# An S5 block with layer norms: the adds of Gelu and residual, moved from GpSimd to VectorE

## Chip, cores and metric

One core of a Trainium2 chip. The metric is the device time of one execution in microseconds (us); lower is better.

## The reference

`x` has 16 batches of 96 channels and 256 positions, in float32. Cut to what is computed:

```python
u = group_norm(x).transpose(0, 2, 1)             # 32 groups of 3 channels
fx = layernorm(u, ln1_g, ln1_b)
Bu = einsum('ph,blh->blp', B_bar, fx)            # 48 complex states
xs = associative_scan(h[t] = lam_bar * h[t-1] + Bu[t])
y = 2.0 * real(einsum('hp,blp->blh', Cc, xs)) + D * fx
y = gelu(y) + fx                                 # the add that the change moves
fy = layernorm(y, ln2_g, ln2_b)
z1, z2 = split(fy @ W_enc.T, 2, axis=-1)
y = (z1 * gelu(z2)) @ W_dec.T + fy
out = x + y.transpose(0, 2, 1)
```

## The kernel before

Channels lie on the 96 partitions. The 16 batches are two halves, H = 0 and 1; a half has 2048 columns, in NT = 4 tiles of 512, and tile i of half H has PSUM bank (H, i). Positions are sorted into T = 8 phases, so that the scan is seven steps between phases and a short doubling over the rest (`Z`). Each engine has its program written out by hand, one list of instructions in a fixed order with semaphore waits, and nothing reorders it. The halves are interleaved: while half 0 is in one stage, half 1 is in an earlier one.

The stages of a half that matter here, with the engine of each:
- TensorE writes the S5 outputs to PSUM: `direct`, `local_outputs`, and last `carried_outputs` (`Z,yl` matmuls in the trace).
- ScalarE takes Gelu of each tile: `gelu_y`, output `gl` (L379), semaphore `gl_ready`.
- The residual `fx` is added: `second_input`, `y2 = gl + fx`. On GpSimd (L290) for tiles 0 and 2 with semaphore `y2_pool`; on VectorE (L982) for tiles 1 and 3 with semaphore `y2_vec`. The inputs are read in order, the output is written with a step of 8 floats, since it goes back from phases to positions. In the trace the output is called `y`.
- TensorE centres y2: `center(H, i)` (`y,mt` matmuls), after it has waited for all four tiles. ScalarE makes `sq` and `xc` of it (`evacuate`), TensorE sums the squares (`variances`, `sq,mt`).
- VectorE works out the reciprocal root: `inverse_sigma(1, H)`, a chain of small instructions on `rs`, `upper` and `parts`. TensorE spreads it: `broadcast` (`parts,bcm`).
- VectorE scales: `scale_tile`, output `fy`, one instruction a tile with one operand from PSUM, semaphore `fy_ready`.
- TensorE's `encode` (`fy,mt`) needs two `fy` tiles for `encode(0, 0)` and four for the rest; then `gelu_z` on ScalarE, `gate` on VectorE (`w<-ps,vecs,y`), `decode` on TensorE, `finish` on VectorE (`sq<-ps,sm,res`), and a store.
- GpSimd makes `res = fy + x` for each tile: `residual` (L298), each waiting for its `fy`. It is the last thing on GpSimd, and in its list stands behind `second_input(1)`.

TensorE's list around the change, which the change leaves in this order:

```python
for i in range(NT - 1):
    direct(1, i); local_outputs(1, i)
pe.wait_ge(y2_pool, 2); pe.wait_ge(y2_vec, 2)
for i in range(NT):
    center(0, i); doubling(1, i)
...
    carried_outputs(1, i)
broadcast(1, 0)
encode(0, 0)
pe.wait_ge(y2_pool, 4); pe.wait_ge(y2_vec, 4)
for i in range(NT):
    center(1, i)
encode(0, 1)
```

Of the kernel before, what the change touches and what calls it, by code (L numbers as in the profile page):

```python
# [34 lines left out]
ALU = mybir.AluOpType  # L35
# [7 lines left out]
T = 8  # L43
# [5 lines left out]
NT = HC // TILE  # L49
RT = TILE // RC  # L50
# [38 lines left out]
def s5_block(nc, x, small, mats, mask_in, out):  # L89
    ctx = ExitStack()  # L90
    with ctx:
        def sb(name, shape, dt=F32):
            return ctx.enter_context(nc.sbuf_tensor(name, shape, dt))

        def sem(name):
            return ctx.enter_context(nc.semaphore(name))
# [3 lines left out]
        gl = sb("gl", [C, 2, HC])  # L100
        xc = sb("xc", [C, 2, HC])
        sq = sb("sq", [C, 2, HC])
        fx = sb("fx", [C + 1, 2, HC])
        w = sb("w", [P2, 2, HC])
        y2 = sb("y2", [C, 2, HC])
# [80 lines left out]
        z_ready = sem("z_ready")  # L186
        y_done = sem("y_done")
        gl_ready = sem("gl_ready")
        y2_pool = sem("y2_pool")
        y2_vec = sem("y2_vec")  # L190
        enc_done = sem("enc_done")
        gz_ready = sem("gz_ready")
# [9 lines left out]
        def cols(t, H, i, p=96):  # L202
            return t[0:p, H, TILE * i:TILE * (i + 1)]
# [7 lines left out]
        def s(c, n=1):  # L211
            return sm[:, c:c + n]

        def m(c, n=96):
            return mt[:, c:c + n]
# [7 lines left out]
        def tbl(k, n=NK, at=0):  # L223
            return tb[:, k, at:at + n]
# [14 lines left out]
        @block.sync  # L239
        def _(sp):  # L240
            for k, (first, last) in enumerate(LOADS):
                if last == B:
                    sp.dma_start(mt[:, N_EARLY:], mats[:, N_EARLY:]).then_inc(in_mats, 16)
                sp.dma_start(xs[:, first:last, :], x[:, first:last, :]).then_inc(in_x[k], 16)
            for n in range(2 * NT):
                H, i = divmod(n, NT)
                sp.wait_ge(out_ready, n + 1)
                sp.dma_start(out[:, 2 * n:2 * n + 2, :],
                             cols(ost, H, i).rearrange("c (n l) -> c n l", l=L)).then_inc(stored, 16)
            sp.wait_ge(stored, 16 * 2 * NT)  # L250

        @block.gpsimd
        def _(pool):
            n = [0]

            def chain(ins):
                n[0] += 1
                ins.then_inc(pool_chain, 1)

            def settle():  # L260
                pool.wait_ge(pool_chain, n[0])

            nc.gpsimd.memset(fx[96:97, :, :], 1.0).then_inc(ones_ready, 1)
            nc.gpsimd.memset(Z[:, :, :, 0:1], 0.0).then_inc(ones_ready, 1)

            pool.wait_ge(cos_ready, 1)
            nc.gpsimd.tensor_tensor(
                rotT[:, :, :], m(M_ID).unsqueeze(1).broadcast_to([96, T, 96]),
                tbl(COS, T).unsqueeze(2).broadcast_to([96, T, 96]), ALU.mult).then_inc(rotcos_ready, 1)
            pool.wait_ge(in_mats, 16)  # L270

            def combine(dst, mat_a, ca, mat_b, cb, n_mats):

                def mat(c):
                    return m(c).unsqueeze(1).broadcast_to([96, n_mats, 96])

                def coef(c):
                    return c.unsqueeze(2).broadcast_to([96, n_mats, 96])

                chain(nc.gpsimd.tensor_tensor(dst[:, 0], mat(mat_a), coef(ca), ALU.mult))  # L280
                chain(nc.gpsimd.tensor_tensor(dst[:, 1], mat(mat_b), coef(cb), ALU.mult))
                settle()
                return nc.gpsimd.tensor_tensor(dst[:, 0], dst[:, 0], dst[:, 1], ALU.add)

            def second_input(H):

                yv = y2[:, H, :].rearrange("c (m b) -> c b m", b=T)
                for i in (0, 2):
                    pool.wait_ge(gl_ready, NT * H + i + 1)
                    nc.gpsimd.tensor_tensor(  # L290
                        yv[:, RT * i:RT * (i + 1), :], cols(gl, H, i).rearrange("c (b m) -> c b m", b=RT),
                        cols(fx, H, i).rearrange("c (b m) -> c b m", b=RT), ALU.add).then_inc(y2_pool, 1)

            def residual(H):

                for i in range(NT):
                    pool.wait_ge(fy_ready, NT * H + i + 1)
                    nc.gpsimd.tensor_tensor(  # L298
                        cols(res, H, i), cols(fy, H, i),
                        xs[:, HB * H + 2 * i:HB * H + 2 * i + 2, :].rearrange("c n l -> c (n l)"),  # L300
                        ALU.add).then_inc(res_ready, 1)

            pool.wait_ge(tables_ready, 1)
            combine(rotX, M_ID, tbl(XCO, NX), M_SW, tbl(XSI, NX), NX).then_inc(rotx_ready, 1)
            combine(yl, M_C, tbl(CU, T), M_CS, tbl(SU, T), T).then_inc(yl_ready, 1)
            pool.wait_ge(yl_ready, 1)
            nc.gpsimd.tensor_tensor(yl[:, 1], yl[:, 0], tbl(RK, T).unsqueeze(2).broadcast_to([96, T, 96]),
                                    ALU.mult).then_inc(yl_ready, 1)
            for H in range(2):
                second_input(H)  # L310
                if H:
                    residual(0)
            residual(1)

        @block.scalar
# [106 lines left out]
        def _(pe):  # L422
# [103 lines left out]
            def local_outputs(H, i):  # L526
                for j in range(RT):
                    b = RT * i + j
                    if b:
                        pe.wait_ge(w_local[H], b)  # L530
                    mm(bank(H, i)[0:96, RC * j:RC * (j + 1)], yl[:, 0, b, :], rcols(w, H, b),
                       start=False, stop=False)
# [8 lines left out]
            def encode(H, i):  # L541

                if H == 0:

                    pe.wait_ge(fy_ready, (2, 4, 4, 4)[i])
                    if i == 2:
                        pe.wait_ge(taken[1], NT + 3)
                    if i == 3:
                        pe.wait_ge(taken[1], 2 * NT)
                        pe.wait_ge(var_read, 4)  # L550
                else:
                    pe.wait_ge(fy_ready, NT + i + 1)
                    pe.wait_ge(out_ready, (1, 2, 3, 4)[i])
                mm(bank(*Z1[H, i])[0:96, :], m(M_WE), cols(fy, H, i))
                mm(bank(*Z2[H, i])[0:96, :], m(M_WE + 96), cols(fy, H, i)).then_inc(enc_done, 1)
# [66 lines left out]
            for i in range(NT - 1):  # L622
                direct(1, i)
                local_outputs(1, i)
            pe.wait_ge(y2_pool, 2)
            pe.wait_ge(y2_vec, 2)
            for i in range(NT):
                center(0, i)
                doubling(1, i)
# [5 lines left out]
                carried_outputs(1, i)  # L635
            broadcast(1, 0)
            encode(0, 0)
            pe.wait_ge(y2_pool, 4)
            pe.wait_ge(y2_vec, 4)
            for i in range(NT):  # L640
                center(1, i)
            encode(0, 1)
# [19 lines left out]
        def _(dve):  # L662
# [168 lines left out]
            def statistics(H, q):  # L831

                for k, (first, _) in enumerate(LOADS):
                    if first == HB * H + q:
                        dve.wait_ge(in_x[k], 16)
                nc.vector.bn_stats(st[:, HB * H + q, :], xs[:, HB * H + q, :]).then_inc(gn_stats, 1)  # L836
# [73 lines left out]
            def scale_tile(k, H, i, dst, gain, ready):  # L910

                dve.wait_ge(inv_bcast[k], NT * H + i + 1)
                stt(cols(dst, H, i), cols(xc, H, i), gain, bank(H, i)[0:96, :],
                    ALU.mult, ALU.mult).then_inc(ready, 1)

            def scan(H, b):

                dve.wait_ge(u_done, NT * H + b // RT + 1)
                if b == 1:
                    dve.wait_ge(w_first, H + 1)  # L920
                else:
                    dve.wait_ge(w_local[H], b - 1)
                stt(rcols(w, H, b), rcols(w, H, b - 1), tbl(RK, 1, 1),
                    bank(H, b // RT)[0:96, RC * (b % RT):RC * (b % RT + 1)],
                    ALU.mult, ALU.add).then_inc(w_local[H], 1)
# [52 lines left out]
            def second_input(H, i):  # L978

                dve.wait_ge(gl_ready, NT * H + i + 1)  # L980
                yv = y2[:, H, :].rearrange("c (m b) -> c b m", b=T)
                nc.vector.tensor_tensor(  # L982
                    yv[:, RT * i:RT * (i + 1), :], cols(gl, H, i).rearrange("c (b m) -> c b m", b=RT),
                    cols(fx, H, i).rearrange("c (b m) -> c b m", b=RT), ALU.add).then_inc(y2_vec, 1)
# [10 lines left out]
                doubled(0, i)  # L995
            for b in range(1, T):
                scan(1, b)
            second_input(0, 1)
            second_input(0, 3)
            for k in range(NDBL):  # L1000
                doubled(1, k)
            inverse_sigma(1, 0)
            second_input(1, 1)
            for i in range(NT):
                if i == 2:
                    second_input(1, 3)
                scale_tile(1, 0, i, fy, s(G2), fy_ready)
            dve.wait_ge(vecs_ready, 1)
            gate(0, 0)
# [78 lines left out]
```

## Time and profile before

| | us |
|---|---|
| runs shown | 110.52, 117.62, 116.42 (median 116.42) |
| the profiled execution's own time | 110.42 |
| its span, first to last instruction | 108.6 |
| TensorE busy | 94.9 |
| VectorE busy | 77.6 |
| ScalarE busy | 41.0 |
| GpSimd busy | 31.9 |

The span is what the profile covers; 1.8 us of the execution's time lie around it. In the rows PE is TensorE's matmuls, PEld its weight loads, DVE VectorE, ACT ScalarE, POOL GpSimd. `L664` and `L424` are lines of helpers that record many operations, so an instruction is told by its tiles. A matmul of float32 operands appears as two instructions. Times are from the span's start.

### The profile page before, as it was taken

To read this page: it belongs to the slowest core of one execution; us is meant where nothing else is said; L and a number is where in the kernel's file an instruction comes from. 1 tells how busy PE (TensorE), PEld (TensorE's weight loads), DVE (VectorE), ACT (ScalarE), POOL (GpSimd) and SP (SyncE) were. 2 spreads that over 40 slices of the span, in tenths; PEclk is the share of its full clock that TensorE was granted. 3 is DMA by queue.
4 is the path that set the end of the run, shared out by engine and by line. 5 is a ranking of instruction groups with operands and counts; after the bars stand their busy time and mean duration, and the time that the engine had idled before them with its cause. 6 is when DMAs were issued, how large, how long until landed. Compare 5 with 4: busy or idle time off the path is not lost.

```text
span 108.6 us, 1488 instructions
## 1 busy us (share of the span) xinstructions
PE 94.9 (87%) x502; PEld 56.2 (52%) x502; DVE 77.6 (71%) x260; ACT 41.0 (38%) x79; POOL 31.9 (29%) x26
## 2 busy tenths in 40 slices
PE   5999897269989929999899999999599999999960
PEld 4668766146555715676476655567324432533310
DVE  1688999999986899658677302389990289994590
ACT  2254167807449100024037009818049722024200
POOL 8600000400049992000018000007995000296000
PEclk9999999955799999999999999999999999999997
DMA  2997000000000000000000000000000000450135
GB/s 77 275 262 168 3 0 0 6 0 0 0 0 0 0 0 3 0 6 0 0 0 0 0 0 3 6 0 0 0 0 0 0 0 0 118 149 29 28 84 177
DMA packets 3767, 3.79 MB, mean 35 GB/s; under 512 B 496, under 2 KB 3664, under 8 KB 3760
## 3 DMA queue, kind: packets, MB, share of 16 engines
q1 hardware_dynamic: 3392, 3.49, 12.3%
q10 hardware_dynamic: 368, 0.20, 0.8%
q8 instruction: 4, 0.07, 0.3%
q14 instruction: 3, 0.02, 0.1%
HBM read 2.12 MB, written 1.57 MB: 34 GB/s over the span
## 4 chain that ended last, share of the span: by engine, by line
PE 70%; DVE 21%; issue 4%; ACT 1%; DVEq 1%
PE ps L424 70%; DVE st L836 2%; DVE fy L664 2%; DVE pm L885 2%; DVE sc L694 2%; DVE rs L664 1%; DVE upper L668 1%; DVE sq L664 1%; DVE tb L664 1%; DVE tb L668 1%; DVE y L982 1%; DVE gn L664 1%; DVE rs L694 1%; DVE fx L664 1%; DVE sc L664 1%
## 5 line engine op out<-in xcount | busy, mean ns | idle before, releaser
L424 PE MATMUL ps<-fy,mt 96*96 96x512 f32 x32 | 14.9, 600 | 1.3 <-DVE fy L664 1.3
L290 POOL TENSOR_TENSOR y<-gl,fx 96x512 f32<-96x512 f32 x4 | 6.1, 1524 | 29.8 <-ACT gl L379 29.8
L298 POOL TENSOR_TENSOR res<-fy,xs 96x512 f32<-96x512 f32 x8 | 10.7, 1359 | 11.6 <-DVE fy L664 11.5
L424 PE MATMUL ps<-xs,pm 96*96 96x256 f32 x32 | 10.8, 492 | 3.3 <-DVE pm L885 3.3
L385 ACT ACTIVATE y<-ps,vecs 96x512 f32<-96x512 f32 x8 | 5.5, 687 | 16.4 <-PE ps L424 16.4
L664 DVE SCALAR_TENSOR_TENSOR w<-ps,vecs,y 96x512 f32<-96x512 f32 x8 | 5.9, 743 | 7.4 <-ACT y L385 7.4
L424 PE MATMUL ps<-fx,dm 96*96 96x512 f32 x16 | 8.4, 605 | 2.6 <-issue 2.2
L933 DVE TENSOR_TENSOR Z<-Z,ps 96x240 f32<-96x240 f32 (+3 forms) x8 | 2.8, 355 | 9.5 <-PE ps L424 9.5
L424 PEld LDWEIGHTS ps<-fy,mt 96*96 96x96 f32 x32 | 5.0, 163 | 8.7 <-issue 6.8
L424 PEld LDWEIGHTS ps<-xs,pm 96*96 96x96 f32 x32 | 6.4, 214 | 5.9 <-DVE pm L885 3.8
L379 ACT ACTIVATE gl<-ps,db 96x512 f32<-96x512 f32 x8 | 5.5, 684 | 9.4 <-PE ps L424 9.4
L424 PE MATMUL ps<-wm 96*96 96x256 f32 x20 | 7.9, 586 | 1.2 <-DVE wm L949 1.2
L424 PE MATMUL ps<-fx,um 97*96 97x256 f32 x32 | 8.2, 390 | 0.2 <-DVE fx L664 0.2
L424 PE MATMUL ps<-w,yl 96*96 96x256 f32 x32 | 8.2, 379 | 0.0
L664 DVE SCALAR_TENSOR_TENSOR w<-w,tb,ps 96x256 f32<-96x256 f32 x14 | 6.6, 471 | 1.9 <-ACT w L366 1.2
L424 PE MATMUL ps<-w,mt 96*96 96x512 f32 x16 | 7.8, 602 | 0.0
L424 PEld LDWEIGHTS ps<-w,yl 96*96 96x96 f32 x32 | 5.2, 163 | 5.1 <-issue 4.0
L358 ACT ACTIVATE sq<-ps,vecs 96x512 f32<-96x512 f32 x8 | 5.5, 686 | 6.2 <-PE ps L424 6.2
L424 PE MATMUL ps<-y,mt 96*96 96x512 f32 x16 | 7.7, 595 | 0.1
L340 ACT ACTIVATE sq<-ps,gn 96x256 f32<-96x256 f32 x16 | 6.5, 470 | 2.7 <-PE ps L424 2.6
L424 PE MATMUL ps<-Z,yl 96*96 96x256 f32 x32 | 7.2, 379 | 0.0
L424 PEld LDWEIGHTS ps<-wm 96*96 96x96 f32 x20 | 5.1, 262 | 3.6 <-DVE wm L949 1.2
(112 smaller groups left out, 168.1 us busy)
## 6 DMA issues: line engine op xcount, KB each, us to landing
out_dram<-sq SPq DMA_DIRECT2D x8, 192.0 KB, 2.2
xs<-x_dram SPq DMA_DIRECT2D x3, 384.0 KB, 6.1
xs<-x_dram SPq DMA_DIRECT2D x2, 192.0 KB, 3.5
mt<-mats_dram SPq DMA_DIRECT2D x1, 338.6 KB, 6.8
mt<-mats_dram ACTq DMA_DIRECT2D x1, 180.0 KB, 3.9
sm<-small_dram ACTq DMA_DIRECT2D x1, 8.6 KB, 2.8
cmask<-mask_dram ACTq DMA_DIRECT2D x1, 9.0 KB, 4.9
```

Of the source, the lines that this page charges most:

```text
L290: nc.gpsimd.tensor_tensor(yv[:, RT * i:RT * (i + 1), :], cols(gl, H, i).rearrange("c (b m) -> c b m", b=RT), cols(fx, H, i).rearrange("c ( ...
L298: nc.gpsimd.tensor_tensor(cols(res, H, i), cols(fy, H, i), xs[:, HB * H + 2 * i:HB * H + 2 * i + 2, :].rearrange("c n l -> c (n l)"), ALU. ...
L340: nc.scalar.activation(t[:, H, :].rearrange("c (b n a) -> c n b a", b=T, n=HB)[:, n], bank(H, n // 2)[0:96, L * (n % 2):L * (n % 2 + 1)].r ...
L358: nc.scalar.activation(cols(sq, H, i), bank(H, i)[0:96, :], ACT.Square, bias=vecs[:, 2:3]).then_inc(squared[1], 1)
L379: nc.scalar.activation(cols(gl, H, i), bank(H, i)[0:96, :], ACT.Gelu, bias=db[:, 0:1]).then_inc(gl_ready, 1)
L385: nc.scalar.activation(cols(gz, H, i), bank(*Z2[H, i])[0:96, :], ACT.Gelu, bias=vecs[:, 1:2]).then_inc(gz_ready, 1)
L424: return nc.tensor.matmul(o, lhsT, rhs, start=start, stop=stop)
L664: return nc.vector.scalar_tensor_tensor(out=o, in0=a, scalar=sca, in1=b, op0=op0, op1=op1)
L668: return nc.vector.tensor_scalar(o, a, s1, None, op0)
L694: self.add(nc.vector.tensor_tensor(*a))
L836: nc.vector.bn_stats(st[:, HB * H + q, :], xs[:, HB * H + q, :]).then_inc(gn_stats, 1)
L933: nc.vector.tensor_tensor(zd, zd, o[:, :, d:], ALU.add).then_inc(z_ready, 1)
```

## The change

VectorE makes all eight y2 tiles. In half 0 it makes the four one after another behind the scan of half 1; in half 1 it makes tile 0 ahead of the first `scale_tile`, and tiles 1, 2 and 3 each ahead of the `scale_tile` with the same number. GpSimd keeps only `residual`, without a `second_input` ahead of it. The semaphore `y2_pool` goes, and TensorE waits for counts 4 and 8 of `y2_vec`. `second_input(H, i)` itself is the same code.

```diff
-            def second_input(H):
-
-                yv = y2[:, H, :].rearrange("c (m b) -> c b m", b=T)
-                for i in (0, 2):
-                    pool.wait_ge(gl_ready, NT * H + i + 1)
-                    nc.gpsimd.tensor_tensor(
-                        yv[:, RT * i:RT * (i + 1), :], cols(gl, H, i).rearrange("c (b m) -> c b m", b=RT),
-                        cols(fx, H, i).rearrange("c (b m) -> c b m", b=RT), ALU.add).then_inc(y2_pool, 1)
...
-            for H in range(2):
-                second_input(H)
-                if H:
-                    residual(0)
+            residual(0)
             residual(1)
...
-            pe.wait_ge(y2_pool, 2)
-            pe.wait_ge(y2_vec, 2)
+            pe.wait_ge(y2_vec, 4)
             for i in range(NT):
                 center(0, i)
                 doubling(1, i)
...
             encode(0, 0)
-            pe.wait_ge(y2_pool, 4)
-            pe.wait_ge(y2_vec, 4)
+            pe.wait_ge(y2_vec, 8)
             for i in range(NT):
                 center(1, i)
...
             for b in range(1, T):
                 scan(1, b)
-            second_input(0, 1)
-            second_input(0, 3)
+            for i in range(NT):
+                second_input(0, i)
             for k in range(NDBL):
                 doubled(1, k)
             inverse_sigma(1, 0)
-            second_input(1, 1)
-            for i in range(NT):
-                if i == 2:
-                    second_input(1, 3)
+            second_input(1, 0)
+            for i in range(NT):
+                if i:
+                    second_input(1, i)
                 scale_tile(1, 0, i, fy, s(G2), fy_ready)
             dve.wait_ge(vecs_ready, 1)
             gate(0, 0)
```

VectorE's list from the end of `inverse_sigma(1, 0)` (output `parts`) to the first two gates (output `w`), before:

```order
L668 TENSOR_SCALAR upper<-rs 128x128
L664 SCALAR_TENSOR_TENSOR parts<-upper,cmask,rs 128x128
L982 TENSOR_TENSOR y<-gl,fx 96x2x256
L664 SCALAR_TENSOR_TENSOR fy<-xc,sm,ps 96x512 x2
L982 TENSOR_TENSOR y<-gl,fx 96x2x256
L664 SCALAR_TENSOR_TENSOR fy<-xc,sm,ps 96x512 x2
L664 SCALAR_TENSOR_TENSOR w<-ps,vecs,y 96x512 x2
```

The same place after the change (`y<-gl,fx` is `second_input`, now L967; `fy` is `scale_tile`):

```order
L649 SCALAR_TENSOR_TENSOR parts<-upper,cmask,rs 128x128
L967 TENSOR_TENSOR y<-gl,fx 96x2x256
L649 SCALAR_TENSOR_TENSOR fy<-xc,sm,ps 96x512
L967 TENSOR_TENSOR y<-gl,fx 96x2x256
L649 SCALAR_TENSOR_TENSOR fy<-xc,sm,ps 96x512
L967 TENSOR_TENSOR y<-gl,fx 96x2x256
L649 SCALAR_TENSOR_TENSOR fy<-xc,sm,ps 96x512
L967 TENSOR_TENSOR y<-gl,fx 96x2x256
L649 SCALAR_TENSOR_TENSOR fy<-xc,sm,ps 96x512
L649 SCALAR_TENSOR_TENSOR w<-ps,vecs,y 96x512 x2
```

The two adds have become four, and each `fy` but the first has an add right ahead of it.

GpSimd's list from its last table product to its end, before (`yl` are tables of the first stage):

```order
L281 TENSOR_TENSOR yl<-mt,tb 96x768
L283 TENSOR_TENSOR yl<-yl 96x768
L307 TENSOR_TENSOR yl<-yl,tb 96x768
L290 TENSOR_TENSOR y<-gl,fx 96x2x256 x4
L298 TENSOR_TENSOR res<-fy,xs 96x512 x8
```

And after:

```order
L279 TENSOR_TENSOR yl<-mt,tb 96x768
L280 TENSOR_TENSOR yl<-mt,tb 96x768
L282 TENSOR_TENSOR yl<-yl 96x768
L297 TENSOR_TENSOR yl<-yl,tb 96x768
L288 TENSOR_TENSOR res<-fy,xs 96x512 x8
```

The four adds are gone, and the first `res` has only the wait for its `fy` ahead of it.

## Rows read from the trace of the kernel before

**Rows 1.** The page, busy time, share of the span and instructions by engine.

```profile
PE 94.9 (87%) x502; PEld 56.2 (52%) x502; DVE 77.6 (71%) x260; ACT 41.0 (38%) x79; POOL 31.9 (29%) x26
```

**Rows 2.** The chain that ended last, in order: start us, us, what.

```profile
73.75 1.25 DVE upper L668
...
79.71 12.55 PE ps L424 x58
```

**Rows 3.** Timeline, half 0: start us, us, engine line op out<-in [idle before <-releaser].

```profile
56.53 1.28 POOL L290 TENSOR_TENSOR y<-gl,fx 96x512 f32<-96x512 f32 x1 [15.03 <-ACT gl L379]
...
57.35 1.41 DVE L982 TENSOR_TENSOR y<-gl,fx 96x512 f32<-96x512 f32 x1 [0.63 <-ACT gl L379]
...
59.08 1.63 DVE L982 TENSOR_TENSOR y<-gl,fx 96x512 f32<-96x512 f32 x1 [0.32 <-ACT gl L379]
...
64.15 1.02 PE L424 MATMUL ps<-y,mt 96*96 96x512 f32 x2
```

**Rows 4.** Timeline, half 1, 72 to 80 us.

```profile
72.68 2.75 PE L424 MATMUL ps<-Z,yl 96*96 96x256 f32 x12
...
73.02 0.23 DVE L668 TENSOR_SCALAR upper<-rs 128x128 bf16<-128x128 f32 x1
...
73.64 1.28 POOL L290 TENSOR_TENSOR y<-gl,fx 96x512 f32<-96x512 f32 x1 [13.87 <-ACT gl L379]
...
73.75 1.24 DVE L668 TENSOR_SCALAR upper<-rs 128x128 bf16<-128x128 f32 x1
...
75.30 1.09 DVE L982 TENSOR_TENSOR y<-gl,fx 96x512 f32<-96x512 f32 x1
75.36 2.03 POOL L290 TENSOR_TENSOR y<-gl,fx 96x512 f32<-96x512 f32 x1 [0.45 <-ACT gl L379]
...
75.44 1.09 PE L424 MATMUL ps<-parts,bcm 128*96 128x128 bf16 x16
...
76.23 1.38 DVE L664 SCALAR_TENSOR_TENSOR fy<-xc,sm,ps 96x512 f32<-96x512 f32 x2
77.35 3.22 POOL L298 TENSOR_TENSOR res<-fy,xs 96x512 f32<-96x512 f32 x2
77.53 2.03 DVE L982 TENSOR_TENSOR y<-gl,fx 96x512 f32<-96x512 f32 x1
...
77.66 1.96 PE L424 MATMUL ps<-fy,mt 96*96 96x512 f32 x4 [1.13 <-DVE fy L664]
...
79.41 0.71 DVE L664 SCALAR_TENSOR_TENSOR fy<-xc,sm,ps 96x512 f32<-96x512 f32 x1
```

**Rows 5.** Instructions by tile (count: shortest/median/longest ns); last, `fy` (us, mean ns).

```profile
L982 DVE TENSOR_TENSOR y<-gl,fx x4: 1091/1516/2032, 57.4 to 77.5; 96x512 f32<-96x512 f32 x4
...
L290 POOL TENSOR_TENSOR y<-gl,fx x4: 1277/1392/2034, 56.5 to 75.4; 96x512 f32<-96x512 f32 x4
...
L298 POOL TENSOR_TENSOR res<-fy,xs x8: 1265/1268/1997, 77.4 to 98.3; 96x512 f32<-96x512 f32 x8
...
L664 DVE SCALAR_TENSOR_TENSOR fy<-xc,sm,ps 96x512 f32<-96x512 f32 x8 | 5.6, 731 | 0.1
```

**Rows 6.** Timeline, the same stage of half 1 in the second layer norm.

```profile
93.23 1.06 PE L424 MATMUL ps<-parts,bcm 128*96 128x128 bf16 x16
...
93.66 0.74 DVE L664 SCALAR_TENSOR_TENSOR fy<-xc,sm,ps 96x512 f32<-96x512 f32 x1
...
94.48 2.59 POOL L298 TENSOR_TENSOR res<-fy,xs 96x512 f32<-96x512 f32 x2 [11.45 <-DVE fy L664]
```

**Rows 7.** Stretches: us, PE busy (instructions), granted clock, DMA share, GB/s.

```profile
20.00:22.00 2.00, 0.00 (x0) 0.94 0.00 0
...
22.00:28.00 6.00, 5.34 (x14) 0.50 0.00 0
...
38.00:40.00 2.00, 0.00 (x0) 1.00 0.00 0
```

**Rows 8.** Timeline, TensorE behind its idle time of 38 to 40 us.

```profile
40.05 1.07 PE L424 MATMUL ps<-fx,dm 96*96 96x512 f32 x2 [2.21 <-issue]
```

More of the change, by code:

```diff
@@ L188, in s5_block @@
         gl_ready = sem("gl_ready")
-        y2_pool = sem("y2_pool")
         y2_vec = sem("y2_vec")
```

## The prediction, made before the changed kernel was run

> **What bounds the kernel now.** I read the page's line of busy times first, then the chain of waits, then the timeline around the two places where y2 is made, and last the granted clock. TensorE is busy 94.9 us of the 108.6 us span [rows 1], so whatever does not delay TensorE costs nothing. The chain [rows 2] names the places where it is not TensorE: one of them is VectorE from 73.75 us to 77.6 us (the end of `inverse_sigma(1, 0)`, an add, two `fy` tiles). After it the chain is TensorE alone for 12.55 us from 79.71 us. So a delay at 79.71 us, the start of `center(1, 0)`, has no idle time behind it that could swallow it, and goes to the end in full. `center(1, 0)` waits for all four adds of half 1; that wait is the term to work out.
>
> **Half 0 of the change: nothing.** In before, two adds of half 0 run on GpSimd and two on VectorE, the last ending at 59.08 + 1.63 = 60.71 us, and TensorE starts `center(0, 0)` at 64.15 us because its own queue gets there only then [rows 3]: 3.4 us of cover. After, VectorE is free of scans at 56.72 us (57.35 less its 0.63 us of idle time), and the last Gelu tile is there by 59.08 us, where VectorE's add had waited for it. Four uncontended adds at 0.93 us from start to start (worked out below) from 56.7 us end at about 60.6 us. I cost this half at 0; the cover would be gone only if an add took over twice its 1.09 us. The replaced semaphore (one wait for two) costs nothing either, since it is met early.
>
> **The price of an add.** The four adds on VectorE took 1.09 to 2.03 us and those on GpSimd 1.28 to 2.03 [rows 5], and the long ones lie over one another [rows 3, 4]. VectorE's add at 57.35 us starts while GpSimd runs until 56.53 + 1.28 = 57.81, and ends at 58.76, 0.95 us after that. The one at 77.53 us starts in GpSimd's first `res` (77.35 + 1.27 = 78.62, 1.27 being the median of rows 5) and ends at 79.56, 0.94 us after. In the other direction GpSimd's add at 75.36 us starts 0.06 us behind VectorE's of 75.30, and ends at 77.40, 1.01 us after VectorE's end. So of two such instructions the later one is held until the first is over, then needs 0.94 us (VectorE) or 1.01 us (GpSimd). An add on VectorE held by nobody is the 1.09 us one at 75.30; the next instruction starts 0.93 us after it, at 76.23, and 0.15 us before a held one's end (79.56, 79.41). The `fy` tiles, with one operand from PSUM, are not held: two in 1.38 us beside GpSimd's add at 76.23, 0.73 us each with starts 0.65 apart.
>
> The Trainium skill states the same ("SBUF — State Buffer", section Who interferes with whom): a VectorE instruction with two SBUF inputs and a GpSimd instruction that reads SBUF exclude each other for a whole instruction, the first to issue winning. The trace agrees, with the 0.94, 0.95 and 1.01 us above.
>
> **Half 1, what goes.** GpSimd's adds at 73.64 and 75.36 us disappear. The first of them held VectorE's `upper` for 1.24 us, where its like at 73.02 took 0.23 [rows 4]. So `parts` is ready at 74.37 us and not 75.38. But that 1.01 us is not won: TensorE is busy with the sixteen `Z,yl` matmuls (twelve of them in 2.75 us, 0.216 apart, the last starting at 75.05), and the broadcast, now at 75.44, can begin one step behind them, at 75.27. The gain is 0.17 us. The first `fy` can then start 0.43 us later, as in the second round (93.23 to 93.66) [rows 6], at 75.70 us. The first add of half 1 fits in front of it, from 74.30 to 75.39, in time that VectorE would otherwise wait.
>
> **Half 1, what comes.** VectorE's order is now fy, add, fy, add, fy, add, fy where it was add, fy, fy, add, fy, fy, with the wait of `center(1, 0)` on the last add. GpSimd, idle at that time, can start `res` as soon as the first `fy` is there, 0.08 us behind its end (93.66 + 0.74 = 94.40, and 94.48) [rows 6], and each `res` reads two SBUF tiles. Step by step, in us:
> - fy 0 from 75.70 to 76.43. Add 1 issues at 76.35 and has SBUF first: to 77.44. `res` 0 issues at 76.51, is held, and ends at 77.44 + 1.01 = 78.45.
> - fy 1 from 77.28 to 78.01. TensorE's `encode(0, 0)` starts at 78.06, now 77.66.
> - Add 2 issues at 77.93, is held by `res` 0 and ends at 78.45 + 0.94 = 79.39. `res` 1 is held by it and ends at 80.40.
> - fy 2 from 79.24 to 79.97. Add 3 issues at 79.89, is held by `res` 1 and ends at 80.40 + 0.94 = 81.34.
> - `center(1, 0)` starts 0.15 us after the last add (79.56 [rows 4] and 79.71 [rows 2]): 81.49, against 79.71. That is 1.78 us later.
> fy 3 starts 0.15 us before the end of add 3 and ends at 81.92 us, early enough for `encode(0, 1)`, which comes behind the eight matmuls of `center(1, i)`, not before 83 us. `gate(0, 0)` and the rest of VectorE's and GpSimd's work move with TensorE. TensorE is idle for about 1.5 us before 78.06 and again for 1.7 us before 81.49.
>
> **Sum.** 0 (half 0) + 1.78 (half 1) = 1.8 us. The profiled execution took 110.42 us for a span of 108.6; I expect a span of 110.4 and a time of 112.2 us. That is 1.6%; about 2% is what a measurement of this kernel can tell from no change. Of the three runs shown one (110.52) lies with the profiled execution, two (116.42, 117.62) are 6 to 7 us above it, and the profile does not show what makes them so; the median, 116.42, is one of these. The change adds the same 1.8 us there, 118.2. I name the level at which the rows were taken, and let the range reach the other.
>
> **Bounds of the price.** Above: GpSimd wins each time, see below. Below: if no add were held, the adds and `fy` tiles follow from 75.70 at 0.65 and 0.93 us, add 3 runs from 79.51 to 80.60, and `center(1, 0)` starts at 80.75, 1.04 us late. If besides an add cost only what an `fy` tile does (0.73, the nearest row with 96x512 elements [rows 5]), add 3 runs from 78.95 to 79.68 and the loss is 0.12 us. A gain is excluded here: two adds more stand ahead of the wait, one of them between fy 0 and fy 1 on which `encode(0, 0)` waits, and the broadcast moves only 0.17 us. I take 1.78, because both ingredients (0.94 after a holder, 1.01 after a holder) were each seen in before with the same instructions.
>
> The Trainium skill has a rule that would give that lowest case ("GPSIMD Engine Reference", section 4.1 Engine selection): elementwise work of two inputs belongs on VectorE, GpSimd being about twice as slow. By it an add would cost half of 1.27 us, 0.64, and the loss would be about 0.1 us. The trace does not agree: 1.09 us on VectorE against 1.28 on GpSimd. A reason is in "Advanced Engine Details and Errata", section SBUF Cachelines: accesses that each land in another 16-byte line pay a penalty, and this add writes y2 with a step of 32 bytes.
>
> **The rivals.**
> - *Adds without collisions, or short ones.* GpSimd's `res` doesn't get in between, or the adds are cheap: +0.1 to +1.0 us, 110.5 to 111.5. For it: uncontended adds exist. Against: nothing else occupies GpSimd, and `fy` is ready before every add.
> - *GpSimd wins the collisions* (the slower side). `res` 0 issues 0.16 us behind add 1; if GpSimd still gets SBUF first, `res` 0 runs to 77.78, add 1 to 78.72, fy 1 to 79.30; `res` 1 from 79.38 to 80.65, add 2 to 81.59, fy 2 to 82.17; `res` 2 from 82.25 to 83.52, add 3 to 84.46; `center(1, 0)` at 84.61, 4.9 us late: 115.3 us. It decides from one lost collision on (some 1.3 us each). Against it stands the pair at 75.30 and 75.36, where a lead of 0.06 us was enough for VectorE.
> - *The clock falls.* TensorE's granted clock fell once to half (1.2 of 2.4 GHz), shortly before 22 us, in a stretch of 2 us without a matmul, and was there from 22 to 28 us. The 2.21 us of idle time before 40.05 left it at full [rows 7, 8]. If it fell after the two idle stretches around 80 us for as long, 6 us, it would cost half of that, 3 us more: 115.2.
> - *The change helps.* The 1.01 us taken off `upper` would have to reach TensorE; it reaches it with 0.17. Faster by more than 2% needs 2.2 us, and no row has them.
>
> **How the numbers follow.** The forecast, two held adds of three: 0.58, own range 111.6 to 112.8. Without collisions or short: 0.20. GpSimd first: 0.11. Clock: 0.07. Helps: 0.04. The 2% bound lies 2.2 us above the profiled 110.42. The forecast's upper tail over it is about 0.10, with the two rivals 0.28 slower; 0.04 faster; 0.68 within 2%. The range goes from 110.6 to 118.8: from the case without collisions, over the slower rivals, to the upper level of executions, 118.2 and a little.
>
> **What would show it.** In the profile after: `upper` at 0.23 us both times; the broadcast within 0.2 us of 75.27; VectorE's adds in half 0 at about 1.09 us each, and in half 1 two of four at about 1.5 us; GpSimd's first two `res` near 2 us; TensorE idle twice between 76.3 and 81.5 us; `center(1, 0)` at 81.5. If `center(1, 0)` starts before 80.8 us the collisions didn't happen, if after 82.5 GpSimd wins them; a granted clock of 0.50 behind 80 us would speak for the third rival. Any difference before 55 us would be none of this change's.

## The result, and the profile after

| | executions | us |
|---|---|---|
| before, in the comparison on record | 4 | 110.52, 110.80, 116.42, 117.62 |
| changed | 4 | 114.41, 114.48, 114.61, 114.86 (median 114.55) |
| ratio on record | | 1.0355, interval 1.0312 to 1.0398 |
| before, all jobs of this study | 78 | mean 112.75 ± 0.19, median 112.4, 110.2 to 118.1 |
| changed, all jobs | 25 | mean 114.49 ± 0.19, median 114.6, 112.6 to 116.4 |

The ratio on record compares only executions within 1.5% of the lowest of their kernel, and of the kernel before that left two, 110.52 and 110.80. By it the change costs 3.9 us; by all executions 1.74 ± 0.27 us in the mean (1.5%) and 2.2 in the median (± is the standard error of a mean). The same ratio in the three later jobs that ran both kernels is 1.022 (interval 1.014 to 1.030), 1.013 (1.006 to 1.021) and 1.018 (1.001 to 1.035). A job is one batch of executions on one chip. The prediction had 1.8 us. The measured time was inside its range; its forecast that the change would stay within 2% did not hold by the ratio on record.

The profiled execution took 114.41 us for a span of 112.6, 4.0 us more than before. The chain of waits of the changed kernel, in order of time (start us, us, what), stands against [rows 2]:

```profile
40.66 8.13 PE ps L411 x26
...
77.99 0.74 DVE fy L649
78.73 0.99 DVE y L967
79.72 0.56 DVE fy L649
80.28 1.39 DVE y L967
81.67 0.56 DVE fy L649
82.23 1.40 DVE y L967
83.62 0.04 issue
83.67 12.58 PE ps L411 x58
```

VectorE's fy and add in turn have become the chain, and TensorE's long piece of 12.55 us is still 12.58 us long, only later. The timeline of the same place answers to [rows 4]:

```profile
74.11 3.62 PE L411 MATMUL ps<-Z,yl 96*96 96x256 f32 x16
...
76.05 0.23 DVE L653 TENSOR_SCALAR upper<-rs 128x128 bf16<-128x128 f32 x1
...
76.58 1.07 DVE L967 TENSOR_TENSOR y<-gl,fx 96x512 f32<-96x512 f32 x1
...
77.56 1.06 PE L411 MATMUL ps<-parts,bcm 128*96 128x128 bf16 x16
...
77.99 0.74 DVE L649 SCALAR_TENSOR_TENSOR fy<-xc,sm,ps 96x512 f32<-96x512 f32 x1 [0.34 <-PE ps L411]
78.65 1.07 DVE L967 TENSOR_TENSOR y<-gl,fx 96x512 f32<-96x512 f32 x1
78.81 7.03 POOL L288 TENSOR_TENSOR res<-fy,xs 96x512 f32<-96x512 f32 x4 [36.71 <-DVE fy L649]
...
80.20 1.47 DVE L967 TENSOR_TENSOR y<-gl,fx 96x512 f32<-96x512 f32 x1
80.33 1.96 PE L411 MATMUL ps<-fy,mt 96*96 96x512 f32 x4 [1.72 <-DVE fy L649]
...
82.15 1.46 DVE L967 TENSOR_TENSOR y<-gl,fx 96x512 f32<-96x512 f32 x1
...
83.67 1.53 PE L411 MATMUL ps<-y,mt 96*96 96x512 f32 x3 [1.37 <-DVE y L967]
```

`upper` is back at 0.23 us, two adds take 1.07 us and two 1.46 to 1.47, GpSimd's four `res` take 7.03 us where four free ones are 5.1, and TensorE is idle twice, 1.72 and 1.37 us.

Three distances place the 4.0 us. E runs from the span's start to the first `Z,yl` matmul of half 1, ahead of everything changed in half 1. D runs from there to `center(1, 0)`, the changed stretch. The tail is the rest.

| us | E | D | tail |
|---|---|---|---|
| before | 71.81 | 7.90 | 28.92 |
| changed | 74.11 | 9.56 | 28.96 |

D has 1.66 us of the loss, E has 2.30. Ahead of the end of E the two profiles differ in two ways. VectorE waited longer for the input (before first, changed second; start us, us, what):

```profile
6.69 0.42 DVE L836 BATCH_NORM_STATS2 st<-xs 96x6 f32<-96x256 f32 x1 [0.45 <-DMA xs<-x_dram]
```

```profile
7.77 0.42 DVE L821 BATCH_NORM_STATS2 st<-xs 96x6 f32<-96x256 f32 x1 [1.28 <-DMA xs<-x_dram]
```

Further on, TensorE's first `fx,dm` matmul starts 0.6 us later than the 40.05 of [rows 8]:

```profile
40.66 1.07 PE L411 MATMUL ps<-fx,dm 96*96 96x512 f32 x2 [3.19 <-issue]
```

The later input is the likely cause of these 0.6 us; no run tests it. And the granted clock was low at another time (stretches: us, PE busy, granted clock; before first, changed second):

```profile
20.00:30.00 10.00, 7.34 (x35) 0.66 0.00 0
30.00:40.00 10.00, 7.54 (x58) 1.00 0.00 0
40.00:50.00 10.00, 9.78 (x51) 1.00 0.01 2
```

```profile
20.00:30.00 10.00, 6.97 (x47) 0.83 0.01 2
30.00:40.00 10.00, 7.17 (x58) 1.00 0.00 0
40.00:50.00 10.00, 9.18 (x40) 0.83 0.01 2
```

Before, the half clock (1.2 GHz) lay between 20 and 30 us: 0.34 of 10 us off the mean are 6.8 us at half clock. Changed, the same 6.8 us lay in two parts, between 20 and 30 us and between 10 and 20, where the mean was also 0.83. A further part lay between 40 and 50, and from 40.66 us on TensorE has hardly any idle time there: 0.17 of 10 us are 3.4 us at half clock, and half of those, 1.7 us, are lost. From `fx,dm` to the end of E took 31.76 us before and 33.45 changed, 1.7 us more. So 0.6 + 1.7 = 2.3 us is E's difference. Whether the change has a part in it was the question for the runs.

### The profile page after: what moved, and what is told of

It reads as the page before. It is cut to its first block, busy times and chain, and to the rows that moved or that the text cites. A ratio compares the mean times of both kernels' runs of the same rounds, so it can differ in the third digit from the quotient of the medians.

```text
span 112.6 us, 1486 instructions
## 1 busy us (share of the span) xinstructions
PE 96.7 (86%) x502; PEld 57.5 (51%) x502; DVE 79.4 (71%) x264; ACT 40.8 (36%) x79; POOL 27.2 (24%) x22
## 4 chain that ended last, share of the span: by engine, by line
PE 65%; DVE 19%; DMA 5%; issue 5%; ACT 1%; SPq 1%; DVEq 1%
PE ps L411 65%; DMA xs<-x_dram 5%; DVE y L967 3%; DVE fy L649 2%; DVE rotT L649 1%; DVE pm L870 1%; DVE sc L679 1%; DVE st L821 1%; DVE rs L649 1%; DVE sq L649 1%; SPq L243 1%; DVE fx L649 1%; DVE sc L649 1%; ACT y L372 1%; DVEq L91 1%
## 5 line engine op out<-in xcount | busy, mean ns | idle before, releaser
L288 POOL TENSOR_TENSOR res<-fy,xs 96x512 f32<-96x512 f32 x8 | 12.1, 1530 | 49.4 <-DVE fy L649 49.3
L411 PE MATMUL ps<-fx,dm 96*96 96x512 f32 x16 | 9.3, 663 | 3.6 <-issue 3.2
L411 PE MATMUL ps<-xs,pm 96*96 96x256 f32 x32 | 9.6, 450 | 2.8 <-DVE pm L870 2.8
L411 PE MATMUL ps<-w,yl 96*96 96x256 f32 x32 | 9.1, 411 | 0.0
L967 DVE TENSOR_TENSOR y<-gl,fx 96x512 f32<-96x512 f32 x8 | 9.0, 1182 | 0.0
L411 PEld LDWEIGHTS ps<-w,yl 96*96 96x96 f32 x32 | 5.7, 178 | 5.9 <-issue 4.9
L411 PEld LDWEIGHTS ps<-xs,pm 96*96 96x96 f32 x32 | 5.8, 193 | 5.0 <-DVE pm L870 3.1
L649 DVE SCALAR_TENSOR_TENSOR fx<-xc,sm,ps 96x512 f32<-96x512 f32 x8 | 5.6, 737 | 3.3 <-PE ps L411 3.3
L821 DVE BATCH_NORM_STATS2 st<-xs 96x6 f32<-96x256 f32 x16 | 6.5, 418 | 1.3 <-DMA xs<-x_dram 1.3
```

Of the source, the lines that this page charges most:

```text
L288: nc.gpsimd.tensor_tensor(cols(res, H, i), cols(fy, H, i), xs[:, HB * H + 2 * i:HB * H + 2 * i + 2, :].rearrange("c n l -> c (n l)"), ALU. ...
L411: return nc.tensor.matmul(o, lhsT, rhs, start=start, stop=stop)
L649: return nc.vector.scalar_tensor_tensor(out=o, in0=a, scalar=sca, in1=b, op0=op0, op1=op1)
L967: nc.vector.tensor_tensor(yv[:, RT * i:RT * (i + 1), :], cols(gl, H, i).rearrange("c (b m) -> c b m", b=RT), cols(fx, H, i).rearrange("c ( ...
```

## The experiments

**The changed kernel again.** No edit.

> The changed kernel once more, nothing edited. Two distances in the profile tell the causes apart. D is from the first Z,yl matmul of half 1 to center(1, 0): 7.90 us before, 9.56 us after. E is from the span's start to that Z,yl matmul, all of it ahead of the changed instructions of half 1: 71.81 us before, 74.11 us after. Theory A (the change itself costs D alone, +1.7 us, and the rest of the loss is where TensorE's clock happened to be low and when the input landed in the one execution): D is 9.5 to 9.6 again, E moves by over 0.5 us from 74.11, times spread. Theory B (the change also slows the first part): E is 74.1 within 0.2 us, the ratio to the kernel before stays near 1.035.

Six executions, mean 114.83 us against 112.25 for 18 of the kernel before in the same job, and the ratio on record fell to 1.022. E was 71.69, even less than before, with the half clock at the place where the kernel before had it (mean 0.66 from 20 to 30 us, 1.00 from 30 to 50), and D 9.56. So E's 2.3 us are not the change's, theory A, and half 0 of the change costs nothing ahead of the end of E either. But the profiled time was 114.42 us again, for another reason, in TensorE's timeline and clock at 80 us:

```profile
77.92 2.15 PE L411 MATMUL ps<-fy,mt 96*96 96x512 f32 x4 [1.71 <-DVE fy L649]
81.25 6.21 PE L411 MATMUL ps<-y,mt 96*96 96x512 f32 x8 [1.19 <-DVE y L967]
87.29 1.88 PE L411 MATMUL ps<-fy,mt 96*96 96x512 f32 x4
```

```profile
79.00:81.00 2.00, 1.06 (x3) 0.64 0.00 0
81.00:83.00 2.00, 1.75 (x2) 0.50 0.00 0
83.00:85.00 2.00, 2.00 (x4) 0.50 0.00 0
85.00:87.00 2.00, 2.00 (x4) 0.65 0.00 0
```

The eight matmuls of `center(1, i)` took 6.21 us where they take 3.67. The clock had fallen between TensorE's two idle stretches: a mean of 0.64 from 79 to 81 us puts the fall at 79.6 us. That is 1.6 us after the first idle stretch had ended and 0.5 us ahead of the second, in the `fy,mt` matmuls, which took 2.15 us for 1.96. The tail was 31.29 us: 2.3 more. This is the prediction's third rival, except that only one of the two idle stretches lay ahead of the fall.

**Half the change each.** `half0` is the kernel before with this edit (the counts of TensorE's waits follow):

```diff
-            for H in range(2):
-                second_input(H)
-                if H:
-                    residual(0)
+            second_input(1)
+            residual(0)
             residual(1)
...
-            second_input(0, 1)
-            second_input(0, 3)
+            for i in range(NT):
+                second_input(0, i)
```

`half1` leaves half 0 to both engines and has the change's loop in half 1:

```diff
-            second_input(1, 1)
+            second_input(1, 0)
             for i in range(NT):
-                if i == 2:
-                    second_input(1, 3)
+                if i:
+                    second_input(1, i)
                 scale_tile(1, 0, i, fy, s(G2), fy_ready)
```

> Only half 0 of the change: VectorE makes the four tiles of half 0, half 1 as before. Theory A: D stays 7.9 us, the time is that of the kernel before in its lower executions, 110.5 to 111, and E is what clock and input give. Theory B, if the cause lies in half 0: time near 112.8 to 113, E near 74.1, D 7.9.

> Only half 1 of the change: VectorE makes the four tiles of half 1 and GpSimd those of half 0 as before. Theory A: D is 9.5 to 9.6 us, times as for the full change. Theory B, if the cause lies in half 0: D 9.5 and time near 112.2.

`half0`: D 7.89 us, tail 28.99, ten executions from 110.41 to 114.48, mean 113.03 ± 0.45 against 112.25 ± 0.30 for the kernel before, and not the 110.5 to 111 us expected. The difference of 0.8 is under two of its own errors, so the mean settles little; D settles it. E was 75.79 in this profile, with the clock at half in two places ahead of 50 us. `half1`: D 9.56 us, E 73.52, mean 114.68 of four, and no half clock at 80 us though TensorE had the same two idle stretches, 1.72 and 1.37 us. The whole of D's growth comes from half 1.

**The residual out of the way.**

```diff
+            pool.wait_ge(y2_vec, 8)
             residual(0)
             residual(1)
```

> The changed kernel, with GpSimd's first residual held back until all y2 tiles are there, so that no res instruction lies over an add. If the held adds are worth what the prediction took (0.46 us each, with 0.27 us more at the third add than the uncontended chain), D falls from 9.56 to about 8.95 (center(1, 0) 1.04 us later than before and not 1.7), adds all at 1.09 us, and the time falls by 0.6 to 0.75 us against the changed kernel. Rival: the order of VectorE's list alone sets D and it stays at 9.5. The res tiles come about 5 us later, which has cover until the first finish.

D 8.78 us, a little below the 8.95 expected. VectorE's part of the timeline in this profile:

```profile
77.10 0.74 DVE L650 SCALAR_TENSOR_TENSOR fy<-xc,sm,ps 96x512 f32<-96x512 f32 x1 [0.33 <-PE ps L412]
77.76 1.07 DVE L968 TENSOR_TENSOR y<-gl,fx 96x512 f32<-96x512 f32 x1
78.67 0.73 DVE L650 SCALAR_TENSOR_TENSOR fy<-xc,sm,ps 96x512 f32<-96x512 f32 x1
79.31 1.08 DVE L968 TENSOR_TENSOR y<-gl,fx 96x512 f32<-96x512 f32 x1
80.22 0.73 DVE L650 SCALAR_TENSOR_TENSOR fy<-xc,sm,ps 96x512 f32<-96x512 f32 x1
80.87 1.08 DVE L968 TENSOR_TENSOR y<-gl,fx 96x512 f32<-96x512 f32 x1
```

Every add is at 1.07 or 1.08 us, so the two long ones came from GpSimd's `res` and cost 9.56 - 8.78 = 0.78 us. The remaining 0.88 us over the 7.90 of before is left to the order of the list; the last experiment tests that. Four executions, 112.91 to 116.71, say nothing finer.

**The write in order.** Left out is the rearrangement from phases to positions; y2 has its columns in another order, and what follows is computed on that.

```diff
-                    yv[:, RT * i:RT * (i + 1), :], cols(gl, H, i)...
+                    cols(y2, H, i).rearrange("c (b m) -> c b m", b=RT), cols(gl, H, i)...
```

> The changed kernel with the adds' output written in order instead of with a step of 8 floats; the rearrangement from phases to positions is left out, so y2 has its columns in another order and everything behind it is computed on that. Theory (the step of 32 bytes makes the add 1.09 us long): uncontended adds take 0.70 to 0.75 us, D falls by 0.6 to 1.1 us from 9.56, since two adds are still held by a res. Rival (two inputs from SBUF make the add long): adds stay at 1.09.

By tile, in this profile (count: shortest/median/longest ns):

```profile
L967 DVE TENSOR_TENSOR y<-gl,fx x8: 679/686/1095, 57.4 to 80.0; 96x512 f32<-96x512 f32 x8
...
L288 POOL TENSOR_TENSOR res<-fy,xs x8: 1255/1269/1719, 77.2 to 99.8; 96x512 f32<-96x512 f32 x8
```

A free add took 0.68 us, the last two, beside GpSimd's `res`, 1.09, and D was 8.63. The step of 32 bytes in the output is worth 0.4 us an add on VectorE; two inputs from SBUF alone don't make it long. This is one execution.

**TensorE kept busy at 80 us.** The changed kernel with dummy matmuls into a free bank:

```diff
+            pe.wait_ge(gl_ready, NT + 1)
+            keep_busy(3, bank(1, 0))        # 3 x mm(free[0:96, 0:256], wm[:, 0:96], wm)
             encode(0, 0)
+            keep_busy(3, bank(1, 0))
             pe.wait_ge(y2_vec, 8)
```

> The changed kernel with six dummy matmul calls (256 columns, float32, 0.43 us each) in TensorE's two idle stretches, three behind broadcast(1, 0) and three behind encode(0, 0), so that TensorE is not idle there. Clock theory (the clock falls to half in part of the executions because of these two stretches, as in the second profile of the changed kernel, where that cost 2.4 us): no stretch of clock 0.50 between 60 us and the end in any profile, D within 0.3 us of 9.56, and the mean over executions falls by 0.5 to 1.5 us against the changed kernel's. Rival (the fall at 80 us is rare and the changed kernel's surplus lies ahead of 60 us): mean unchanged within 0.3 us, or worse by the matmuls.

> The changed kernel with six dummy matmul calls in the two idle stretches, again. Clock theory: no clock 0.50 between 60 us and the end, mean 1.2 to 2 us above the kernel before (D's share alone, 1.66), below the changed kernel.

> The changed kernel once more, in one job with the filled one. So far D has been 9.55 and 9.56 us in its two profiles, and the clock fell at 79.6 us in one of them. Clock theory: mean over the executions 0.5 to 1.5 us above the filled kernel's in this job, and 2 to 3 us above the kernel before; D 9.5 to 9.6. Rival: no difference to the filled kernel beyond 0.3 us.

In both profiles D was 9.58 to 9.59, the tail 28.93 to 28.96, with no half clock behind 60 us. `again2`, unfilled, had D 9.56 and the fall at 81.6 us (tail 31.17). The means: filled 113.99 and 114.20 us in two jobs of twelve executions, together 114.09 ± 0.26; changed 114.49 ± 0.19. The difference of 0.40 ± 0.32 has the expected sign and is not clear of noise. What was expected of the means in that job failed: the changed kernel was 1.0 us above the kernel before (114.42 against 113.38 of 17) and not 2 to 3, and 0.2 above the filled one and not 0.5 or more; the filled one was 0.8 above the kernel before and not 1.2 to 2.

**How often the clock falls there.**

> The changed kernel, one profile more. D 9.5 to 9.6 us. If the clock falls near 80 us, the distance from center(1, 0) to the end of the span is 31.3 us and not 28.9; I expect this in one profile of three.

> The changed kernel, a third job. D 9.56 us. If the clock falls near 80 us in about half of the executions, as in two of four profiles so far, the mean is 2.8 us above the kernel before; if in a quarter, 2.2; if the fall is an accident of two profiles, 1.7.

> One profile more of the changed kernel, for the share of executions in which the clock falls near 80 us: center(1, 0) to the end 28.9 us without a fall, 31.2 with it; D 9.56.

> One profile more of the changed kernel, as the run before it.

> The kernel before, one profile more. D 7.9 us, no clock fall between 60 us and the end, 28.9 us from center(1, 0) to the end; E anywhere from 71.7 to 76 us, with the early clock falls at other places than in the first profile.

| profile | E | D | tail |
|---|---|---|---|
| changed | 74.11 | 9.56 | 28.96 |
| again | 71.69 | 9.56 | 31.29 |
| again2 | 73.92 | 9.56 | 31.17 |
| again3 | 75.26 | 9.56 | 28.93 |
| again4 | 74.40 | 9.56 | 28.95 |
| again5 | 73.30 | 9.56 | 28.99 |
| again6 | 72.77 | 9.56 | 28.96 |
| before | 71.81 | 7.90 | 28.92 |
| before2 | 74.90 | 7.90 | 28.90 |

Two of seven profiles of the changed kernel have the fall at 80 us, neither of the kernel before. In `again2` (mean 0.66 from 81 to 83 us) it lies as in `again`: 1.5 us after the first idle stretch, in the `fy,mt` matmuls (2.31 us for 1.96), ahead of the second stretch. With `half1`, which has the same two stretches, it is two of eight. D is the same to 0.01 us in each. E goes from 71.7 to 75.3 with the changed kernel and from 71.8 to 74.9 with the kernel before: the two overlap. Two of seven times 2.3 us are 0.6 us on average, which with D's 1.66 gives 2.3 us. The pooled means have 1.74 ± 0.27 and the medians 2.2. `again4` (mean 114.36 of six, the kernel before 112.39 of 16 in that job) lies between the lower two of its three cases. `before2` shows besides that the kernel before falls to half clock at `fx,dm` too, the place where the prediction saw it stay at full [rows 7, 8]:

```profile
40.04 1.99 PE L424 MATMUL ps<-fx,dm 96*96 96x512 f32 x2 [1.88 <-issue]
```

```profile
40.00:50.00 10.00, 9.96 (x37) 0.68 0.01 2
```

The idle time was 1.88 us here, shorter than the 2.21 us of the first profile.

**The early idle time filled.** The kernel before, with dummy matmuls in the idle stretches that end at 22.66 and 40.05 us:

```diff
                 variances(0, 0, i)
+            pe.wait_ge(bias_ready, 1)
+            keep_busy(5, bank(1, 1))
             center_batch(1, 0)
...
+            pe.wait_ge(taken[0], 2 * HB)
+            keep_busy(4, bank(1, 3))
             pe.wait_ge(dm_ready, 1)
```

> The kernel before with dummy matmul calls of the same kind in its two early idle stretches: five behind the variances of half 0 (idle 2.9 us before 22.66), four ahead of the wait for the output tables (idle 2.2 us before 40.05). If the scatter of both kernels (E from 71.7 to 75.8 us in the profiles) comes from clock falls after these two stretches, the executions draw together near the lowest, 108 to 110.5 us, and the profile has no 0.50 between 15 and 60 us. Rival (the scatter comes from when the input lands): it stays at 3 us and more.

Four of six executions were at 110.02 to 111.40, the others 116.82 and 122.28. The profile was of the longest:

```profile
19.00:36.00 17.00, 17.00 (x82) 0.51 0.01 1
36.00:53.00 17.00, 17.00 (x66) 0.50 0.01 1
53.00:60.00 7.00, 6.83 (x39) 0.98 0.00 0
```

TensorE's rows show a matmul all the time, and the clock stayed at half for 34 us. So the expectation failed: four executions drew together, but all except one above the 108 to 110.5 us expected, and the fall that the dummies were to prevent came all the same, in matmuls, soon after 19 us. The ratio on record is 0.988 (interval 0.981 to 0.995), from the low executions; the mean of all six is 113.7 us. E was 83.61 us in this profile against 71.81. TensorE's matmuls at 17 us began only 0.24 us later than in the profile of before, so nearly all of the 11.8 us come from the half clock and the dummies themselves, not from the input.

**Another order.** VectorE: add, add, fy, fy, add, add, fy, fy; `residual` behind all adds, as above.

```diff
-            second_input(1, 0)
             for i in range(NT):
-                if i:
+                if i % 2 == 0:
                     second_input(1, i)
+                    second_input(1, i + 1)
                 scale_tile(1, 0, i, fy, s(G2), fy_ready)
```

> The changed kernel with VectorE's half 1 in the order add, add, fy, fy, add, add, fy, fy, and GpSimd's residual behind all adds. Theory (the order of the list and the held adds make D): encode(0, 0) waits for fy 1 only, as before; add 3 ends 7.67 us after the first Z,yl matmul and D is 7.8 to 7.9, so TensorE is idle once, for 1.2 us, and the clock stays up at 80 us; the time is that of the kernel before within 0.5 us, 1.5 to 3 us below the changed kernel. Rival: four adds on VectorE cost by their number, D stays above 8.7 as with the residual held back alone.

> The order add, add, fy, fy again, in one job with the changed kernel. Theory (D and the idle time at 80 us are all that the change costs): D 7.7 us, no clock fall between 60 us and the end, mean over the executions that of the kernel before within 0.5 us and 1.5 to 2.5 us below the changed kernel's in the same job. Rival (VectorE's eight adds cost something outside D): mean above the kernel before by over 0.5 us.

Timeline of `pairs`:

```profile
74.05 3.62 PE L412 MATMUL ps<-Z,yl 96*96 96x256 f32 x16
...
76.51 2.02 DVE L968 TENSOR_TENSOR y<-gl,fx 96x512 f32<-96x512 f32 x2
...
78.37 1.38 DVE L650 SCALAR_TENSOR_TENSOR fy<-xc,sm,ps 96x512 f32<-96x512 f32 x2
79.67 2.01 DVE L968 TENSOR_TENSOR y<-gl,fx 96x512 f32<-96x512 f32 x2
79.80 1.96 PE L412 MATMUL ps<-fy,mt 96*96 96x512 f32 x4 [1.25 <-DVE fy L650]
...
81.74 3.67 PE L412 MATMUL ps<-y,mt 96*96 96x512 f32 x8
```

D 7.70 and 7.69 us in the two profiles, 0.2 below the kernel before, though VectorE makes all eight tiles. `pairs` had expected 7.8 to 7.9. Against the 8.78 of `res_late`, which differs in the order alone, one `fy` fewer (0.65 us from start to start) stands ahead of the last add, and the second add uses the 0.33 us in which VectorE waited for the broadcast: together 0.98 of the 1.08 us. TensorE is idle only ahead of `fy,mt`. 24 executions have a mean of 112.50 ± 0.24 us, 2.0 ± 0.3 below the changed kernel and 0.25 ± 0.3 below the kernel before. The ratios to the kernel before were 0.9958 (0.990 to 1.001) and 1.0072 (1.002 to 1.012) in the two jobs. It is no faster than the kernel before by any amount that can be measured; it undoes the loss. The rival, a cost of over 0.5 us of VectorE's eight adds outside D, falls: in the job of `pairs2` the mean was 112.50 us against 112.39 for the kernel before.

## Why the prediction was right or wrong

- *Half 0 costs nothing*: right in the profile. The four adds took 3.89 us from 58.94, all near 1.1 us, and `center(0, 0)` started at 66.44, 3.6 us after them. `half0` left D at 7.89. One reading was off: four adds from 56.7 us use up the cover until 64.15 when an add takes about 1.95 us, not "over twice its 1.09".
- *`upper` gives 1.01 us to VectorE and 0.17 to TensorE*: right. It took 0.23 us; the broadcast came 3.45 us after the first `Z,yl`, before 3.63.
- *The price of an add and who holds whom*: right. Free adds 1.07, held ones 1.46 and 1.47 (forecast 1.46 and 1.45 by its own start and end times), VectorE first at add 1. `res_late` took the collisions away and got 0.78 us back, where the prediction's own bound said 0.74.
- *`center(1, 0)` 1.78 us late*: D says 1.66. The term was 0.12 us too large, most of it because `center(1, 0)` began 0.06 us after the last add's end (83.61 and 83.67) and not 0.15. The rival in which GpSimd wins the collisions, 4.9 us, did not come in any profile.
- *Adds at half of GpSimd's price, no collisions*: by the trace no. `plain_write` shows what that rival's low price needs: an output in order, 0.68 us. The Trainium skill ("Advanced Engine Details and Errata", section SBUF Cachelines) states a penalty for accesses that each land in another 16-byte line. The run agrees, with 1.07 us at a step of 32 bytes against 0.68.
- *The tail moves as a whole*: right where the clock stays up, 28.9 us in every such profile.
- *The clock rival*: this is a step that failed. It was held to 0.07, from one idle stretch of 2.21 us that left the clock at full. That row was one draw: in `before2` the clock fell at the same place around a stretch of 1.88 us. At 80 us it fell in two of seven profiles, in the matmuls behind the first idle stretch of 1.7 us. It costs 2.2 to 2.3 us, less than the 3 of the prediction.
- *The level*: the other step that failed, and the one on which "0.68 within 2%" rested. The sum set its 1.8 us on 110.42 us, the profiled execution, and put what differs between executions ahead of 55 us at nothing, but for an upper level of 116 to 118 that it left unexplained. 78 executions of the kernel before have a median of 112.4 us; 110.42 is below all but three of them. 72 of them fill the stretch from 110.2 to 114.5 without a gap, and only six lie at 116.3 to 118.1. Where profiles exist (E from 71.7 to 75.8, `fill_early` aside), the half clock lay at different times ahead of 50 us, and the changed kernel has the same scatter. In the comparison on record, four executions of it at 114.4 to 114.9, none near its own lowest of 112.59, stood against two of before that are among the lowest eight of 78. That makes 3.9 us of a difference that is 1.7 to 2.3. For the profiled execution the rest is E's 2.3 us; the other three have no profile, so what made them long stays open.

So the mechanism and the size of its term stood. That the measured time fell into a range 8.2 us wide, 110.6 to 118.8, says little for them; D says more. Whether the change is within 2% depends on which executions are compared: 1.5% by the means, 2.0% by the medians, 3.6% by the ratio on record, 1.3 to 2.2% by the same ratio in the later jobs.

Open: why the clock falls at 80 us in some executions only, and how often beyond two in seven. The second idle stretch is not what makes it fall, since both falls came ahead of it. That the first, longer than in the kernel before (1.72 against 1.13 us), is needed is argued and not shown: it rests on filled profiles without a fall (two), on profiles of `pairs` (two) and of before (two), and with a share of two in seven, six profiles without a fall could also be chance. The gain of the filled kernel, 0.40 ± 0.32 us, doesn't settle it.

## What to carry to other kernels

Moving work to the engine that does it faster (here 1.09 us an add against 1.28) gains nothing when the consumer waits for the last piece and that piece comes later. Look at the position of each piece in the receiving engine's list against the waits on the others, and put it where that engine waits anyway. Taking work off an engine also sets it free to start its next work earlier, here `residual`, straight into the stretch where it holds up the moved instructions. To judge a change of 1 to 2% in a kernel whose executions scatter by 5%, measure the distance between two events around the change in several profiles; it repeated to 0.01 us where the time did not to 4 us.

## What the runs showed of the hardware that was not expected

- An output written with a step of 32 bytes makes a 96x512 float32 add on VectorE 1.07 to 1.09 us long, against 0.68 in order; GpSimd took 1.28 with the step and, for `res`, 1.27 without [rows 5].
- The granted clock stayed at 0.50 from 19 to 53 us in one execution (`fill_early`) while the rows show matmuls without idle time, and in `again6` the mean was 0.65 from 30 to 40 us with TensorE busy for 10.00 of the 10 us. TensorE busy by its rows did not by itself bring the clock back.
- The length of a single idle stretch did not tell whether the clock falls. It fell in two of seven profiles of the changed kernel 1.5 to 1.6 us after an idle stretch of 1.7 us, in matmuls, and in `before2` in a stretch of 1.88 us (mean 0.74 from 39 to 40 us, with no matmul); around stretches of 2.21 us (before) and 2.25 us (`again`) it stayed at full.
